# Six of eight state pairs of a selective scan summed on GpSimd, and three queues reordered around them, in a one-core transformer kernel

## The reference, cut to what matters

```python
    x = x + _L0_xattn_ref(ctx_1024, _layernorm(x), wq, wk, wv)      # softmax attention over the context
    x = x + _L0_attn_ref(_layernorm(x), W_in, ..., A_log, B_mat, C_mat, D_vec)
    # second block: proj = x @ W_in.T + b_in ; x_t, delta = split(proj) ; delta = relu(delta)
    #   h = h * exp(A * delta_t) + (x_t * delta_t) * B ; y_t = h @ c0     (16 states per channel)
    #   out = sigmoid(x @ W_gate.T + b_gate) * (y + x_t * D_vec) @ W_out.T + b_out
    x = x + _L1_xattn_ref(_layernorm(x), ctx, ctx, ...)              # keys: relu, cubed and renormalised;
    #   kv = sum_j k_j v_j and ksum = sum_j k_j over the context rows j
```

## Time and profile before

| | before |
|---|---|
| median of 3 runs | 2303.12 us (2297.48 to 2305.03) |
| the profiled execution, its own time | 2306.15 us |
| its span | 2304.4 us |
| busy: PE | 1885.3 us, 82% |
| busy: DVE | 1593.4 us, 69% |
| busy: ACT | 1474.6 us, 64% |
| busy: POOL | 1207.8 us, 52% |

### The profile page before, as it was taken

How to read it: one execution, slowest core, us unless ns; L and a number is a source line. 1 busy time by engine, 2 the same in 40 slices (tenths; PEclk the granted TensorE clock), 3 DMA queues, 4 the chain that set the end, 5 groups by cost and what they waited for, 6 DMA issues and landing times. The chain is left out here.

```text
span 2304.4 us, 41527 instructions
## 1 busy us (share of the span) xinstructions
PE 1885.3 (82%) x14324; PEld 1272.6 (55%) x14355; DVE 1593.4 (69%) x2945; ACT 1474.6 (64%) x3431; POOL 1207.8 (52%) x1300
## 2 busy tenths in 40 slices
PE   4898898888888888888888885368888888888864
PEld 2655555555555555555555542246666666766642
DVE  3347677677677677677666678536888888878863
ACT  2557777776776776776776777313666666666654
POOL 1435545545545544545445443336776766767751
PEclk9998999999999999999999988768988988889886
DMA  7321122122112112111112110100000000000000
GB/s 187 103 88 58 42 67 67 42 67 67 51 58 67 47 66 65 58 54 65 58 44 65 37 64 0 52 10 8 13 11 11 11 11 11 11 14 11 10 9 10
DMA packets 48370, 103.20 MB, mean 45 GB/s; under 512 B 6384, under 2 KB 25072, under 8 KB 43376
## 3 DMA queue, kind: packets, MB, share of 16 engines
q1 hardware_dynamic: 48240, 101.57, 13.9%
HBM read 93.03 MB, written 8.52 MB: 44 GB/s over the span
## 5 line engine op out<-in xcount | busy, mean ns | idle before, releaser
L856 POOL TENSOR_TENSOR kcube<-kcube,ksq 128x512 f32<-128x512 f32 x128 | 178.0, 1391 | 542.2 <-ACT ksq L713 542.2
L691 ACT ACTIVATE abuf<-delta,cols 128x496 f32<-128x496 f32 x512 | 335.3, 698 | 31.1 <-DVE gP L938 28.4
L866 POOL TENSOR_TENSOR yac<-yac,gP 128x1024 f32<-128x1024 f32 x128 | 301.4, 2355 | 11.4 <-ACT gP L700 10.3
L938 DVE TENSOR_TENSOR_SCAN gP<-abuf,ps_s 128x512 f32<-128x512 f32 x256 | 293.5, 1199 | 0.6 <-POOL yac L866 0.6
L512 PE MATMUL ps_kv<-w_k,cT 128*128 128x256 f32 x1024 | 283.4, 424 | 0.0
L938 DVE TENSOR_TENSOR_SCAN gL<-abuf,ps_s 128x512 f32<-128x512 f32 x192 | 223.1, 1205 | 54.0 <-ACT abuf L691 52.4
L524 PE MATMUL ps_kv<-kcube,cx 128*128 128x256 f32 x1024 | 246.5, 384 | 8.6 <-ACT kcube L731 7.8
L512 PEld LDWEIGHTS ps_kv<-w_k,cT 128*128 128x128 f32 x1024 | 202.5, 208 | 59.1 <-issue 32.4
L580 PE MATMUL ps_kv<-hT,w_pT 128*128 128x512 f32 x384 | 191.0, 621 | 48.9 <-ACT delta L764 45.0
L524 PEld LDWEIGHTS ps_kv<-kcube,cx 128*128 128x128 f32 x1024 | 194.9, 193 | 59.9 <-issue 28.2
L567 PE MATMUL ps_t<-gL,diag 128*128 128x512 f32 x384 | 185.3, 607 | 15.4 <-DVE gL L938 13.1
(11 more groups left out here) (312 smaller groups left out, 4399.0 us busy)
## 6 DMA issues: line engine op xcount, KB each, us to landing
cT<-in_h_ctxT SPq DMA_DIRECT2D x32, 1028.0 KB, 5.0
cx<-in_ctx SPq DMA_DIRECT2D x32, 1024.0 KB, 5.3
xT<-in_h_xT SPq DMA_DIRECT2D x8, 512.0 KB, 4.0
xcur<-in_x SPq DMA_DIRECT2D x32, 128.0 KB, 2.0
x_mid<-xb SPq DMA_DIRECT2D x16, 256.0 KB, 2.2
x_c<-x_mid SPq DMA_DIRECT2D x32, 128.0 KB, 2.0
out<-y SPq DMA_DIRECT2D x32, 128.0 KB, 1.7
kv_all<-vleft SPq DMA_DIRECT2D x8, 256.0 KB, 10.9
```

The lines of the kernel that those rows point to most:

```text
L691: act.activation(abuf[q % 2][:, i, :].rearrange("p (b t) -> p b t", t=T)[:, :, 1:T], delta[J % 2][:, :].rearrange("p (b t) -> p b t", t=T) ...
L856: pool.tensor_tensor(t[:, :, :], t[:, :, :], ksq[:, :, :], ALU.mult).then_inc(S["k3_ready"], 1)
L866: pool.tensor_tensor(yac[:, :, :], yac[:, :, :], pool_home(q)[:, :, :], ALU.add).then_inc(S["pacc_done"], 1)
L938: dve.tensor_tensor_scan(dst[:, i, :], abuf[q % 2][:, i, :], ps_u[:, :], 0.0, ALU.mult, ALU.add).then_inc(S["scan_done"], 1)
```

## The change

Pair 6 goes from TensorE to GpSimd: ACT weighs it just behind the decays of pair 0, and GpSimd adds it behind pair 5. GpSimd adds pair 4 ahead of `pool_ratio`, and pairs 2 and 3 ahead of the last cube. ACT computes `pr` right behind the decays of pair 7. TensorE transposes `pr` between delta and x, does the values ahead of pair 7, and no longer waits for `ks_added` ahead of the scores, since the transposed key sums now go through the bank `ps_m`; it waits for it ahead of the transposes of `lnh` instead. DVE copies `pT` right behind `plm` and forms `o_sb` ahead of `yg`.

```diff
@@ -29,7 +29,7 @@
...
 NPAIR = NST // 2
-BY_POOL = (1, 2, 3, 4, 5)
+BY_POOL = (1, 2, 3, 4, 5, 6)
 BY_PE = tuple(q for q in range(NPAIR) if q not in BY_POOL)
@@ -491,7 +491,7 @@
...
         if G >= 2:
-            pe.wait_ge(S["ks_added"], G - 1)
+            pe.wait_ge(S["kse_ready"], G - 1)
         if G:
@@ -541,7 +541,7 @@
...
         if G:
-            pe.wait_ge(S["ks_added"], G)
+            pe.wait_ge(S["kse_ready"], G)
         if G + 1 < NG:
@@ -552,8 +552,11 @@
...
         pe.wait_ge(S["kse_ready"], G + 1)
+        pe.wait_ge(S["hT_ready"], G + 1)
+        if G + 1 < NG:
+            pe.wait_ge(S["x_added"], G + 2)
         for c in range(DC):
-            last = pe.transpose(ps_f[:, D + c * P:D + (c + 1) * P], kse[:, c * P:(c + 1) * P], ident[:, :])
+            last = pe.transpose(ps_m[:, c * P:(c + 1) * P], kse[:, c * P:(c + 1) * P], ident[:, :])
         last.then_inc(S["kst_full"], 1)
@@ -599,19 +602,14 @@
...
             pe.wait_ge(S["lnh_ready"], C + 1)
+            if C:
+                pe.wait_ge(S["ks_added"], C)
             for dc in range(DC):
...
             pe_project(pe, "delta", J)
-
-        if J is not None:
-            pe_project(pe, "x", J)
-        if Z is not None:
-            pe_states(pe, Z, 6)
-        if C is not None:
-            pe_gram(pe, C, 2)
 
@@ -621,14 +619,13 @@
...
             pe.transpose(ps_m[:, 2 * P:3 * P], plm[:, :], ident[:, :]).then_inc(S["pT_full"], 1)
+        if J is not None:
+            pe_project(pe, "x", J)
+        if C is not None:
+            pe_gram(pe, C, 2)
+
+        if A is not None:
             pe_keys(pe, A, 1)
-        if Z is not None:
-            pe_states(pe, Z, 7)
-        if C is not None:
-            pe_gram(pe, C, 3)
-            pe_key_sums(pe, C)
-
-        if A is not None:
             pe.wait_ge(S["pT_ready"], A + 1)
@@ -639,6 +636,12 @@
...
                       skip_group_check=True).then_inc(S["pv_full"], 1)
+        if Z is not None:
+            pe_states(pe, Z, 7)
+        if C is not None:
+            pe_gram(pe, C, 3)
+            pe_key_sums(pe, C)
+
         if J is not None:
@@ -752,6 +755,12 @@
...
             act_decay(act, Z, 7)
+        if A is not None:
+            act.wait_ge(S["negm_ready"], A + 1)
+            if A:
+                act.wait_ge(S["pT_full"], A)
+            act.activation(pr[:, :], ps_s[:, 0:L], ACT.Exp, bias=negm[:, 0:1], scale=rstd0[:, 0:1],
+                           accum_out=rsum[:, 0:1]).then_inc(S["p_ready"], 1)
         if C is not None:
@@ -768,12 +777,6 @@
...
 
-        if A is not None:
-            act.wait_ge(S["negm_ready"], A + 1)
-            if A:
-                act.wait_ge(S["pT_full"], A)
-            act.activation(pr[:, :], ps_s[:, 0:L], ACT.Exp, bias=negm[:, 0:1], scale=rstd0[:, 0:1],
-                           accum_out=rsum[:, 0:1]).then_inc(S["p_ready"], 1)
         if J is not None:
@@ -782,6 +785,8 @@
...
             act_decay(act, J, 0)
+        if Z is not None:
+            act_weigh(act, Z, 6)
         if A is not None:
@@ -868,14 +873,15 @@
...
         g, sc = G % SG, G // SG
+        if Z is not None:
+            pool_add(pool, Z, 4)
         if C is not None:
             pool_ratio(pool, C, 1)
-        if Z is not None:
-            pool_add(pool, Z, 4)
         if A is not None:
...
             pool_add(pool, Z, 5)
+            pool_add(pool, Z, 6)
         if A is not None:
@@ -883,17 +889,17 @@
...
             pool_cube(pool, A, 2)
+        if J is not None:
+            pool_add(pool, J, 2)
+        if A is not None:
             pool.wait_ge(S["x_var"], A + 1)
...
         if J is not None:
-            pool_add(pool, J, 2)
+            pool_add(pool, J, 3)
         if A is not None:
...
                 pool_rstd0(pool, A + 1)
-        if J is not None:
-            pool_add(pool, J, 3)
-        if A is not None:
             if sc >= 2 and g % 2 == 0:
@@ -978,6 +984,10 @@
...
                               ALU.mult).then_inc(S["plm_ready"], 1)
+            dve.wait_ge(S["pT_full"], A + 1)
+            if A:
+                dve.wait_ge(S["pv_full"], A)
+            dve.tensor_copy(pT[:, :], ps_m[:, 0:3 * P]).then_inc(S["pT_ready"], 1)
         if J is not None:
@@ -990,10 +1000,10 @@
...
             dve_keys(dve, A, 1)
-            dve.wait_ge(S["pT_full"], A + 1)
+            dve.wait_ge(S["pv_full"], A + 1)
             if A:
-                dve.wait_ge(S["pv_full"], A)
-            dve.tensor_copy(pT[:, :], ps_m[:, 0:3 * P]).then_inc(S["pT_ready"], 1)
+                dve.wait_ge(S["oT_full"], A)
+            dve.tensor_scalar(o_sb[:, :], ps_m[:, 0:D], rinv[:, 0:1], None, ALU.mult).then_inc(S["o_ready"], 1)
 
@@ -1008,11 +1018,6 @@
...
                                      op1=ALU.mult).then_inc(S["yg_ready"], 1)
-        if A is not None:
-            dve.wait_ge(S["pv_full"], A + 1)
-            if A:
-                dve.wait_ge(S["oT_full"], A)
-            dve.tensor_scalar(o_sb[:, :], ps_m[:, 0:D], rinv[:, 0:1], None, ALU.mult).then_inc(S["o_ready"], 1)
         if J is not None:
@@ -1072,7 +1077,7 @@
...
             dve.wait_ge(S["kst_full"], C + 1)
-            sums = ps_f[:, D:2 * D].rearrange("p (c b k) -> p b c k", c=DC, b=GB)[:, :, :, 0]
+            sums = ps_m[:, 0:D].rearrange("p (c b k) -> p b c k", c=DC, b=GB)[:, :, :, 0]
             ks = ks_all[:, C * GB:(C + 1) * GB, :]
```

## The result

| | before | changed |
|---|---|---|
| median, 17 runs each | 2304.43 us | 2309.0 us (2300.93 to 2316.73) |
| ratio, 95% interval | | 1.0021 (1.0011 to 1.0031) |
| span of the profiled execution | 2304.4 us | 2305.7 us |

What follows compares the result with a forecast made beforehand. It took waits between queues, chiefly `rinv` for `pr`, to bound the kernel. From 2306.15 us, 46.0 gained, 17.5 (clock) and 5.4 (tail) back give 2283.1; less 3.0 to the median, 2280 us, range 2254 to 2306.

Steps and rivals of the forecast that it cites:

- GpSimd's other moves: Pair 4 ahead of `pool_ratio`, pairs 2 and 3 ahead of the last cube: in GpSimd's idle time, cost 0.
- What bounds the kernel: Before the change: waits between queues set the pace, the largest of VectorE being `rinv` for `pr`, 5.1 us a step.
- the second part: The part-by-part account of the change: the `rinv` wait goes, and VectorE waits some 5 us before `yg`.
- `yg` 10.1 us after `dx`: Ordinary step: two weights on ACT and GpSimd's sixth sum lengthen this way from 6.53 to 10.1 us.
- `dx` 3.7 us earlier: Ordinary step: with scores and `pr` sooner, `dx` comes at 1094.7 against 1098.37.
- L1009 back to 0.69, L1007 held by 0.3: VectorE at `yg`: the second cube no longer slows L1009 (1.64 us) but holds L1007; net gain 0.65 us.
- The clock, 17.5 us back: TensorE's 3.5 us idle before the x projection may halve its clock: 1.0 us a step lost, 0.5 for g = 1.
- The strict rival: TensorE's clock falls in every such gap: 39.9 us lost in place of 17.5, 2302 us; chance 0.13.
- `plm` held by GpSimd's power: Rival: `plm` waits for the power of `pool_ratio`, 0.95 us a step, 2300 us; chance 0.06.
- g = 0 shorter by 1.4: Steps with g = 0: TensorE, the bound, loses 1.88 us, less about 0.4 for a wait on key scaling.
- Tail, 1.8 a step: Steps 33 to 35, without attention: `yg` waits for weights and sixth sum, 5.4 us back in all.
- The rival on the slower side: `dx` to `yg` 3.55 us longer, paid only by earlier `dx`; slow clock and held `plm` give 2321 us; chance 0.11.

Runs made afterwards that it cites:

- e1: The changed kernel with `nbias` as a tensor_scalar (one tensor input, a scalar operand) instead of a scalar_tensor_tensor: 2282.02 us, ratio 0.9915.
- e4: The changed kernel with GpSimd's power `rstd1` put behind its sum of pair 3, so that `nbias` waits for that sum: 2320.99 us, ratio 1.0071.
- e3: The kernel before with pair 6 alone moved to GpSimd, and GpSimd's order behind the third cube as in the change: 2417.51 us, ratio 1.0464.
- e5: e1 with GpSimd's sum of pair 5 ahead of the first cube: 2259.86 us, ratio 0.9804.
- e7: e5 plus five needless matmuls filling TensorE's idle time before the transposes of `pr` (g not 0): 2232.73 us, ratio 0.9678.

## Why the prediction was wrong, point by point

In short: the price put at nothing for GpSimd's other moves was wrong. Mean length of a step from row maxima to row maxima, steps 5 to 30, in us:

| g | before | changed | e1 | forecast of the change |
|---|---|---|---|---|
| 1 | 39.83 | 41.72 | 39.49 | -1.15 |
| 2 | 41.07 | 40.39 | 39.51 | -0.86 |
| 3 | 41.88 | 41.38 | 40.63 | -0.86 |
| 0 | 49.49 | 46.82 | 47.47 | -1.4 |

In these 26 steps the changed kernel is 10.5 us shorter than before, and e1, without the hold, 32.9; the forecast has 27.6. Before and behind them the changed kernel loses 11.8 us, where the forecast has 5.4. So of the 24 us that the forecast is off in the profiled executions (23.1 less forecast, 1.3 more measured), 22 go with the hold, and the other errors nearly cancel.

- **What bounds the kernel** held: the wait of `rinv` went, and `yg` with GpSimd behind it took its place, as the second part said.
- **`yg` 10.1 us after `dx`**: right. In the step shown it is 1098.54 - 1088.28 = 10.26 us.
- **`dx` 3.7 us earlier**: not in every step. Counted from the row maxima it comes 4.6 us earlier in the mean of g = 2 and 3, and `yg` 0.9 instead of 0.15. With g = 1 it is 2.0 us earlier only, since `dx` came sooner there before (9.5 us after the row maxima in four of seven steps, against 11.4 to 12.2 with g = 2), and `yg` comes 1.8 us later. The forecast took the chain of g = 2 for g = 1 as well; even in e1 these steps gain 0.3 us, not 1.15.
- **L1009 back to 0.69, L1007 held by 0.3**: right, 0.69 and 0.96. The trace agrees with the Trainium skill there (SBUF — State Buffer, "SBUF: two separate sides"): two SBUF inputs of VectorE and an instruction of GpSimd that reads SBUF exclude each other for the whole instruction. L1017 started 0.40 us before the end of the cube (1098.40 to 1099.67) and took 0.27 longer; the key tile L953, with one input in SBUF and one in PSUM, kept its 0.66 us beside a sum (1112.48).
- **"GpSimd's other moves ... fall in its idle time ...; I take 0"**: this is the step of the prediction that failed. It asked only whether GpSimd had time for the sum of pair 3, not who runs beside it. The same rule that I applied to `yg` applies to `nbias`, which has two SBUF inputs and is released by the very instruction that the moved sum follows. The term was 0 and is 2.14 us of hold in 22 steps. Its net price is 27 us by the medians (2309.0 against e1's 2282.02) and 24 by the ratios, less than 47, mainly since part of the clock term vanished with it; the rest of the difference wasn't looked into. That e1 lies at the forecast of 2280 is partly luck: g = 1 gave much less than forecast there, g = 0, 2 and 3 more. The same lock also gave something back that the forecast hasn't: `kv_all` (L1063, before L1058), another instruction with two SBUF inputs, went from a median of 750 to 373 ns.
- **The clock, 17.5 us back**: about right in size once the hold is gone. In the changed kernel itself it cost little: the gap before the transposes of `pr` was only 1.0 us in the step shown, the low clock fell on gram and delta, and 4 of 17 x projections were slow (2.82 to 3.01 us), all of them with g = 1, for which the forecast had the smaller share. With e1 7 of 17 were (2.92 to 3.62); filling the gap gave 8 to 14 us and, with the sum of pair 5 ahead, 27. The strict rival, the full price in every such gap, isn't borne out. Nor is the lower end that the forecast took from rows 9 and 10, that the clock stays behind an idle time of 2.65 us. In the same trace the clock was granted at 0.54 from 862.30 to 865.00, behind the same idle time:

```profile
862.30 5.38 PE L590 MATMUL ps_kv<-w_oT,yg 128*128 128x256 f32 x16 [2.65 <-DVE xb L954]
```

It happened in one of six such steps before, in none of six in the changed kernel and in all six in e4. So the length of the idle time alone doesn't tell whether the clock falls.
- **`plm` held by GpSimd's power**: no. It takes 0.27 us in all 32 steps, in the step shown with the power (L851, 1084.35 to 1086.00) beside it. What the prediction derived from the Trainium skill for this rival isn't borne out here; whether a long sum would hold `plm` no run shows.
- **g = 0 shorter by 1.4**: it is shorter by 2.6 (46.81 us from row maxima to row maxima against 49.44), while the step behind it, g = 1, got longer, 42.03 against 38.89: 2.14 us of that are the hold, and the slow x projection has most of the rest.
- **Tail, 1.8 a step**: 1.87 of wait, and 2.1 to 2.3 in the step's length. The last `yg` still came 4.8 us sooner (L1019 at 1451.81, L1009 at 1456.61). Of this nothing is left at the end: the output projection behind it ran at the low clock (granted 0.50 from 1452.60 to 1456.00),

```profile
1452.56 6.42 PE L593 MATMUL ps_kv<-w_oT,yg 128*128 128x256 f32 x16 [2.24 <-DVE yg L1019]
```

against 3.72 us before; up to the start of the second loop that and a slower load cost 4.6 us, and the second loop, which is the same in both, took 1.5 us more. The latter was not looked into. No term of the forecast covers either.
- **The rival on the slower side** named the held VectorE, but at the wrong instruction (`plm`). Its reasoning that only the earlier `dx` pays for the 3.55 us fits e3, where `dx` isn't earlier and the time is 4.6% longer, though the held `nbias` has a share in that.
- **The range**: its lower end is a sum gone wrong by 2 us. 2262.5 less 21 x 0.3 is 2256, not 2254.

## What to carry to other kernels

When an instruction moves into idle time of GpSimd, look at what VectorE runs beside it, not only at GpSimd's queue: a tiny instruction with two SBUF inputs that waited for GpSimd was held by GpSimd's next long one in all 22 steps in which that one was under way when it started. The form with one tensor and a scalar operand was not held (e1). One input alone is no guarantee: `diag` has one and took 1292 ns once. And where two ways of equal length lead to the same point, moving work from one to the other gives nothing; both have to be shortened (e5 and e7), and moving it back is no test of what it costs.

## What the runs showed that I had not expected

A 128x1 instruction of VectorE was held for 2.29 us by one GpSimd sum of 2.36 us, while the same arithmetic with a scalar operand ran beside it in 0.21 us. The same idle time of 2.65 us was followed by a projection of 3.69 us in one step and of 5.38 in another. And five needless matmuls of 128x256 a step, in a gap of some 3 us, made a kernel faster by 1.2% (e7 against e5).
